# A three-layer edge-attention kernel: the fetched column goes between a slot's edge product and its scores, and its bank is emptied ahead of the sums

## The reference, cut to what matters

```
f   = leaky_relu(nf[src] @ W_ni + nf[dst] @ W_nj + ef @ W_fij + bias, 0.2)   # E x (4 heads x 32)
e   = sum over d of f * attn                                                  # E x 4
a   = softmax of e over the edges of one destination
h   = sum over those edges of (nf @ W_node)[src] * a                          # N x 4 x 32
nf  = mean of h over heads ;  ef = mean of f over heads
```

## Time and profile before

| what | value |
|---|---|
| three timed runs | 3021.41, 3011.55, 3023.02 us, median 3021.41 us |
| profiled execution | 3008.55 us, span 3006.7 us from first to last instruction |
| mean granted TensorE clock | 0.843 of full speed |
| busy: TensorE matmul | 2404.8 us (80%) |
| busy: VectorE | 2490.5 us (83%) |
| busy: ScalarE | 1447.6 us (48%) |
| busy: GpSimd | 2058.9 us (68%) |

### The profile page before, as it was taken

One profiled execution on the slowest core, in us unless ns is written; L12 is line 12 of the kernel. 1 busy time (PEld: TensorE's weight loads), 2 busy tenths in 40 slices (PEclk: granted clock), 3 DMA queues, 4 the chain that ended last, 5 costly groups with the idle time before them and its releaser, 6 DMA issues.

```text
span 3006.7 us, 50077 instructions
## 1 busy us (share of the span) xinstructions
PE 2404.8 (80%) x15871; PEld 1878.0 (62%) x16027; DVE 2490.5 (83%) x6428; ACT 1447.6 (48%) x3416; POOL 2058.9 (68%) x2167
## 2 busy tenths in 40 slices
PE   3388888888887378888888887649999888998984
PEld 1366667676764356667766665337777777776753
DVE  7399999999997468998999998637888888879784
ACT  0155555555555135555556555414445454445452
POOL 6777777777770577777777776377776666667653
PEclk9699988888899589987999999857778787778796
DMA  6235454535342324343435342332333343333222
GB/s 252 64 96 156 122 147 116 152 110 158 110 128 85 112 74 142 119 149 110 157 111 158 110 153 98 118 103 67 100 120 99 98 136 98 108 108 100 91 92 81
DMA packets 139275, 353.92 MB, mean 118 GB/s; under 512 B 43895, under 2 KB 96027, under 8 KB 120207
## 3 DMA queue, kind: packets, MB, share of 16 engines
q1 hardware_dynamic: 67216, 296.09, 27.9%
q0 software_dynamic: 68960, 39.71, 8.6%
q10 hardware_dynamic: 2838, 14.91, 1.3%
HBM read 137.79 MB, written 212.77 MB: 117 GB/s over the span
## 4 chain that ended last, share of the span: by engine, by line
PE 39%; DVE 29%; issue 14%; ACT 9%; POOL 5%; DMA 3%; SPq 1%; DVEq 0%; ACTq 0%; POOLq 0%
DVE U L1349 12%; PE f_ps L695 12%; PE pick_ps L664 10%; PE f_ps L704 9%; PE xT_ps L685 5%; DVE rows L1266 4%; DVE lr L1277 4%; DVE U L1334 3%; POOL rows L554 2%; ACT f_low L850 2%; ACT xT L841 2%; ACT up L901 2%; PE f_ps L714 2%; ACT wide_ps L889 1%; DVE rows L1378 1%
## 5 line engine op out<-in xcount | busy, mean ns | idle before, releaser
L554 POOL DMA_INDIRECT rows<-nf_tab,src_sb x1995 | 1889.3, 947 | 706.9 <-issue 574.9
L704 PEld LDWEIGHTS f_ps<-w_out,lr 128*128 128x128 f32 x4836 | 701.0, 210 | 379.0 <-issue 277.3
L664 PE MATMUL pick_ps<-nf_part,z 125*128 125x160 bf16 x6345 | 630.0, 264 | 258.4 <-issue 217.0
L1349 DVE TENSOR_TENSOR_SCAN U<-wide_ps,U 128x272 f32<-128x272 f32 (+2 forms) x1272 | 801.6, 694 | 3.2 <-ACT wide_ps L889 2.4
L695 PE MATMUL f_ps<-xT,w_edge 97*128 97x512 f32 x1212 | 753.8, 708 | 22.6 <-ACT ef_new L872 12.0
L664 PEld LDWEIGHTS pick_ps<-nf_part,z 125*128 125x128 bf16 x6345 | 564.6, 112 | 289.8 <-issue 241.3
L704 PE MATMUL f_ps<-w_out,lr 128*128 128x36 f32 (+1 forms) x4836 | 649.8, 274 | 31.2 <-DVE lr L1277 28.8
L1277 DVE TENSOR_TENSOR lr<-f_ps,f_low 128x512 f32<-128x512 f32 x606 | 410.0, 677 | 252.4 <-ACT f_low L850 247.0
L850 ACT ACTIVATE f_low<-f_ps 128x512 f32<-128x512 f32 x606 | 361.0, 596 | 495.9 <-PE f_ps L695 495.9
L685 PE MATMUL xT_ps<-ident,rows 128*97 128x128 f32 x2418 | 431.8, 305 | 76.8 <-issue 37.2
L841 ACT ACTIVATE xT<-xT_ps 97x512 f32<-97x512 f32 x606 | 358.8, 592 | 147.8 <-PE xT_ps L685 145.6
(11 more groups left out here) (163 smaller groups left out, 1070.5 us busy)
## 6 DMA issues: line engine op xcount, KB each, us to landing
u_tab<-up SPq DMA_DIRECT2D x144, 1088.0 KB
s_nd<-edge_first SPq DMA_DIRECT2D x48, 768.0 KB
rows<-nf_tab,src_sb POOLq DMA_INDIRECT x1995, 2.5
ef_tab<-ef_new SPq DMA_DIRECT2D x32, 768.0 KB
ef_st<-ef_tab SPq DMA_DIRECT2D x32, 768.0 KB
z<-fifth_tab SPq DMA_DIRECT2D x141, 96.0 KB
edge_first<-s_nd ACTq DMA_DIRECT2D x16, 768.0 KB
ef_st<-in_edge_attr_dram SPq DMA_DIRECT2D x16, 672.0 KB
```

What stands on the lines that cost most here:

```text
L554: eng.indirect_dma_start(rows[q % RING][:, c * K:c * K + D], None, nf_tab[:, :], bass.IndirectOffsetOnAxis(ap=src_sb[:, t:t + 1], axis=0)) ...
L664: mm = eng.matmul(pick_ps[:, i * PB:(i + 1) * PB], hot[m % 2][0:NQ, f * PW + i * P:f * PW + (i + 1) * P], nf_part[a][0:NQ, f * PB:(f + 1) ...
L704: mm = eng.matmul(f_ps[n % 2][:, u * m:(u + 1) * m], lr[y][:, u * P:(u + 1) * P], w_out[l][:, 0:m], start=True, stop=True)
L1349: last = eng.tensor_tensor_scan(uh[:, c0 * w:c1 * w], dbc[h % 2][:, 0:(c1 - c0) * w], uh[:, c0 * w:c1 * w], 0.0, ALU.mult, ALU.add)
```

## The change

TensorE's list: `pick(b, i)` goes from the place between `turn(g+2)` and `edges(g+1)` to the place between `edges(g+1)` and `scores(g)`. The filler matmuls of the other slots keep their place ahead of `edges`. VectorE's list: `pick_rows(b+3)` of slot i = 2 goes from behind the two `add_up` to right behind `leaky(g+1)`, ahead of them. No instruction is added or removed, and no wait changes.

```diff
                         b, i = g // GB + 2, g % GB
-                        if g >= 0 and i < PICK and b < NPICK:
-                            pick(b, i)
-                        elif g >= 1:
+                        fetch = g >= 0 and i < PICK and b < NPICK
+                        if g >= 1 and not fetch:
                             warm(g + 1, FILL_STEADY)
                         if g + 1 >= 0:
                             edges(g + 1)
+                        if fetch:
+                            pick(b, i)
                         if g >= 0:
                             scores(g)
...
                         leaky(g + 1)
+                        if g >= 0 and i == PICK - 1 and b + 3 < NPICK:
+                            pick_rows(b + 3)
                         if b >= 0:
                             if i == 0:
                                 soften(b)
...
                                 add_up(b, 3)
-                        if g >= 0 and i == PICK - 1 and b + 3 < NPICK:
-                            pick_rows(b + 3)
                         if g >= 0 and i == 0 and b + 4 < NPICK:
                             make_hot(b + 4)
```

## The result

The changed kernel takes 3416.75 us (median of four runs, 3414.78 to 3418.53) beside 3016.48 us for the kernel before: a ratio of 1.133 (95% interval 1.129 to 1.137), 400 us slower. The forecast was 3115 us; the sign was right, the size a quarter of what came. The profiled execution took 3415.36 us, its span is 3413.5 us.

The account below looks back on a forecast made before the run. VectorE was taken to set the pace, losing time to TensorE at the lower clock. New holes of 60 us plus 45 us for the clock made 105 us on 3008.55, forecast 3115 us, range 3000 to 3195.

Parts of the forecast that it names:

- Part one: VectorE, `pick_rows` ahead of the sums: leaky step of slot i = 3 at +6.10, new hole 0.75 or 1.4 us.
- Part two: TensorE, `pick` behind `edges`: edge product at about +6.35, 0.15 to 0.6 us later, behind holes of 2.8 or 3.1 us.
- the clock term: TensorE's clock falls in the 15 subtiles without scans of two layers, 1.5 us each: 45 us; third layer nothing.
- The sum: 60 us of holes left after absorption plus 45 us for the clock: 105 us on the profiled 3008.55 us.
- the third: Rival: TensorE's clock falls in every subtile, first two layers run at the third's 18.3 us; 3150 to 3210 us; chance 0.14.
- The signs that the prediction named: Leaky step of slot i = 3 before +5.4 refutes part one; third stretch's clock above 0.85 refutes the clock term.
- What absorbs the holes: VectorE's present waits for half-clock TensorE absorb part of its new holes, leaving 24, 24 and 12 us by layer.
- Rival 1: TensorE's clock holds, one dense burst after one hole; subtile 16.7 us, 88 us gained, 2920 us; chance 0.18.
- Rival 4: VectorE's `pick_rows` waits 0.8 us for `pick` in all half-clock subtiles: 48 us more, about 3160; chance 0.05.

Follow-up runs that it names:

- e3: Changed kernel plus 12 filler matmuls of 512 columns on TensorE between `turn` and `edges` in slot i = 0; 3024.30 us, ratio 1.002 to the kernel before.
- e10: Changed kernel, but in slot i = 0 `pick` stands ahead of `edges` as before; slots 1 and 2 as changed; 3072.33 us, ratio 1.027 to the kernel before.
- e11: Changed kernel, but only slot i = 0 has the changed order; slots 1 and 2 have `pick` ahead of `edges`; 3419.84 us, ratio 1.142 to the kernel before.
- e7: Changed kernel plus 4 filler matmuls on TensorE between `turn` and `edges` in slot i = 0; 3095.45 us, ratio 1.026 to the kernel before.
- e1: Kernel before with only VectorE's part, `pick_rows` ahead of the sums, TensorE's order unchanged; 3084.83 us, ratio 1.024 to the kernel before.

## Why the prediction was right or wrong

**Part one was right in its mechanism.** The leaky step of slot i = 3 was put at +6.10 and stands at +6.11; the hole on VectorE was put at 1.4 us without scans and 0.75 with them, and is 1.49 and 0.66. The mean of both was put at 0.97 us a subtile; with the clock held (e3) the leaky step of slot i = 3 waits 0.92. The other steps wait too: 52.3 us in 41 subtiles make 1.28 each.

**Part two was right in its mechanism.** The edge product was put at +6.35 and stands at +6.46; the hole was put at 2.8 us without scans and 3.1 with them, and is 2.66 and 2.67. The larger wait that takes the place of the bank's is there.

**The step that failed is the clock term.** The sum let only the 15 subtiles without scans of two layers fall, at 1.5 us each, 45 us, and took nothing for the third layer. From the third subtile of each layer on all those that fetch by `pick` fall, and the lower clock lasts some 10.2 us in each; the subtile grows from 16.9 and 18.3 us to 20.48. That is 3.6 x 88 = 317 us in the first two layers, where the sum had 24 + 24 + 45 = 93 us, and 2.2 x 44 = 97 us in the third, where it had 12. Two errors made this. First, I took each hole by its length alone and let the subtiles with scans keep their present falls. The long hole comes in all subtiles, and with `pick` behind it the clock stays down longer: e10 and e11, which differ in the order of `pick` and `edges`, took 3072 and 3420 us. What the trace shows, 0.51 and 0.99 by turns, is known from longer waits: the Trainium skill ("TensorE: Matmul & The Clock Gate", section "HAM oscillation — how this bites in real kernels") describes a loop whose wait for a DMA, about 3 to 5 us by its figure, lets each iteration start at the throttled clock. Here 2.66 us in each subtile were enough.

Second, the rival that had it, the third, was priced from a mean: 18.3 us, the third layer's subtile, is a mean over subtiles of 15.1 to 20.7 us. The slot at half clock was at hand, 6.09 us. An edge product at +6.35, one such slot, one of half and half ((6.09 + 3.25)/2 = 4.67), and the 1.7 us from edge product to leaky step would have given 18.8 us. Of the rest, 1.2 us stand behind `lay_out` in the trace above, which I did not follow when `take_scores` moved behind `pick`; but e11 has the same length without that, so this sum does not explain why it is 20.48 us. The signs that the prediction named did not warn of it either: the leaky step came at +6.11 and the third stretch's clock was 0.75, both on the side that it called right.

**What absorbs the holes** was moot: where TensorE is at half clock it sets the pace, and VectorE waits 643.3 us where it waited 247.0.

**Rival 1** (the clock holds in one dense burst) was wrong in this kernel. With the hole filled (e3) the clock does hold, 1.00 in the stretch shown, but a subtile then takes 17.3 us, not the 16.7 of its sum, which had only the hole of slot i = 3 beside the busy time. **Rival 4** didn't occur: `pick_rows` starts 0.6 us behind the leaky step's start (794.35 to 794.96), with no wait.

## What to carry to other kernels

Before moving a step out of an engine's idle time, ask what that idle time will be without it: a step that fills a part of a wait can be worth more than its own length where the engine's clock falls in the wait (here 3072 against 3420 us for a step of 1.2 us). Where two engines hand work back and forth in fixed order, look for the instruction that stands between them in a third list (here the two `widen`); with these moved, TensorE's part of the change took the time from 3030 to 2932 us, and VectorE's part added nothing. And price a rival from the slot in its bad state, not from a mean over good and bad.

## What the runs showed of the hardware that was not expected

The clock's fall and the program's own period can keep step: in the changed kernel subtiles of 20.47 to 20.49 us follow each other for tens in a row, in three layers whose score products differ in width. In e11, whose order differs, single subtiles last 20.3 to 20.6 us, and their mean is 20.49 in all layers. That the two hold each other in place is a reading of this, not shown.

And the length of a hole does not fix what follows. A hole of 2.64 us in e7 left the clock up; 2.56 us in e1 was followed by some 3 us at the lower clock, 2.44 us in the same run by 10, and 2.66 us in the changed kernel by a lower clock until 10 us later. In the changed kernel the clock is down before the first matmul behind the hole (2.04 us for the edge product), in e1 only after it (1.10 us). What decides between these no run here settles.
